# Exponentials of a decoder's attention as powers on GpSimd, and block limits in two-source steps on VectorE

## The chip, the cores and the metric
The kernel runs on one core of one Trainium2 chip. The metric is the device time of one execution in microseconds, the median of several runs. The engines of the core work from queues of their own and meet at semaphores: TensorE (PE in the profile), VectorE (DVE), ScalarE (ACT), GpSimd (POOL), and SyncE (SP), which issues the DMAs.

## The reference
A decoder of two layers works on `x`, 4 sequences of 512 rows with 512 features. Layer 0 is a state-space mixer, a cross attention over `ctx` and a feed-forward on selected rows. Layer 1 is what the change touches:

```python
# L1 attention: x is read as (seq=4, batch=512, hidden): 4 positions for each of 512 columns
scores = einsum('bhqd,bhkd->bhqk', q, k) / sqrt(32)      # 16 heads of 32, 4 key/value heads
scores = where(causal, scores, -inf)
attn   = einsum('bhqk,bhkd->bhqd', softmax(scores), v)
x = x + attn @ weight_proj.T
# L1 cross step: each block of 128 features of layernorm(x) is rounded to fp8 by its own limit
amax = max(abs(block)); safe = maximum(amax, 1e-4)
q    = (block * (448 / safe)).astype(float8_e4m3fn);   x = x + (q * safe / 448) @ quantised(ctx).T
# L1 feed-forward: rows rounded to int8, weights ternary
x = x + bitlinear(silu(bitlinear(n, w1)) * bitlinear(n, w3), w2)
```

Because the reference reads the first axis as time, attention has only four positions. A row of sequence s attends to s + 1 keys, and with 16 heads it has 16, 32, 48 or 64 scores.

## The kernel before, in words
`x` lies in SBUF as 16 tiles of 128 rows by 512 features. The last stages (from about 736 us to the end of the span) do the whole of layer 1 as one software pipeline. Tiles are taken in the order of `order`, so that tile n has position s = n % 4. Every engine runs one loop of NT + 15 = 31 turns (NT is 16), and in each turn it does a fixed list of steps on tiles of different age: in VectorE's loop `t2` is the tile two turns behind, `t3` the next older one, and so on. GpSimd's and ScalarE's loops count seven turns later, so their `t9` is the tile that VectorE calls `t2`. No planner orders this at run time. The list of steps in each loop is the order, and an instruction that waits holds everything behind it in its engine's queue.

The way of one tile: `turn_du` and `qkv_product` (PE), `keep_qkv` (ACT, L2185), the products of queries and keys on VectorE (`attend_scores`, L1576) for even positions and on GpSimd (`attend_odd`, L2681) for odd ones. Then `attend_softmax` on VectorE: a sum over 32 features (L1588), the largest score of each head (L1591), and the difference (L1594), which gives the third `at_step`. ScalarE's `exp_keys` (L2191) waits for that and writes the exponentials, which `at_exp` signals. `attend_weights` on VectorE waits for `at_exp`, sums them (L1602), inverts (L1605) and multiplies (L1607). In VectorE's list two steps stand between the difference and `attend_weights`: `add_down` (L1727) and `add_to_x(t3, "attended")` (L1632), the latter on the product of the attention that TensorE made for the tile before. Behind `attend_weights` stands `e_fp8` (L1280 to L1288), whose result ScalarE scales (`scale_eu`, L2256) and TensorE turns (`turn_eu`, L466). Then come the next turn's `f_scale`, `f_gate`, `attend_add`, `h_scale`, `e_scales`, `attend_scores` and so on.

GpSimd's list in one turn is: `minus_mean(t7, 0)`, `minus_mean(t12, 2)`, `minus_mean(t10, 1)` (all L2726), `deviation(t12, 2)` (L2734 and a power, L2737), `attend_part(t9, 1)` (L2702), `deviation(t7, 0)`, `attend_begin` (L2692), `attend_part(t9, 2)`, `deviation(t10, 1)`, `attend_part(t9, 3)`, `attend_last` (L2710), `f_gains` (L2747), `attend_odd`, `h_gain`, `e_back`. `minus_mean(t10, 1)` waits for `x_attended`, which is signalled by the `add_to_x(t3, "attended")` that stands in VectorE's list directly ahead of `attend_weights`. TensorE's list is `e_product`, `turn_o`, `f_down`, `attend_out`, `f_up`, half of `qkv_product`, `turn_eu`, the other half, `turn_du`.

The limits of the fp8 blocks are made in `e_scales` on VectorE: the largest magnitude of each of four blocks (L1643), times the row's scale and not under 1e-4 (L1647, a one-source step), a reciprocal (L1649), and times the scale and 448 (L1651, one-source). All four write 128x4 or less.

ScalarE works with tables of functions: where the next function is not in the loaded table, the program has an ACT_TABLE_LOAD. In the last stages the functions are Exp (L2191), Silu (L2210), Square, Identity and Copy.

Of the kernel before, what the change touches and what calls it, by code (L numbers as in the profile page):

```python
# [13 lines left out]
ALU = mybir.AluOpType  # L14
ACT = mybir.ActivationFunctionType
# [3 lines left out]
P = 128  # L19
BATCH, SEQ, D = 4, 512, 512  # L20
NT = BATCH * SEQ // P
TPB = SEQ // P
KD = D // P
# [12 lines left out]
AH, AKV, AHD = 16, 4, 32  # L36
# [4 lines left out]
ASCALE = float(AHD) ** -0.5  # L41
# [5 lines left out]
FP8_MAX = 448.0  # L47
# [15 lines left out]
def behind(n, lags):  # L63

    return [n - lag if 0 <= n - lag < NT else None for lag in range(lags)]
# [77 lines left out]
def decoder_kernel(nc, x_in, ctx_in, ctxT_in, mask_in, win_in, wout_in, d_in, dtb_in, alog_in, bw_in, cw_in,  # L143
                   lnw_in, lnb_in, wr_in, br_in, w1_in, b1_in, w2_in, b2_in, wqkv_in, wproj_in,
                   f1_in, f2_in, f3_in, out):
    with ExitStack() as top:
        signals = {}

        def sig(name):
            name = HANDED_ON.get(name, (name, 0))[0]  # L150
            if name not in signals:
                signals[name] = top.enter_context(nc.semaphore(name))
            return signals[name]
# [11 lines left out]
        fixed = Region(nc, -(-nc.sbuf_base // 32) * 32, top_end)  # L165
        x = fixed.ring("x", NT, [P, D])
        ident, ones = fixed.one("ident", [P, P]), fixed.one("ones", [P, 1])
        mhalf = fixed.one("mhalf", [P, 8])
        b_sum = fixed.one("b_sum", [P, NT])


# [202 lines left out]
        def spread(name, number, shape, dt=F32, parts=work):  # L374

            made = []
            for k in range(number):
                part = next(p for p in parts if p.end - p.at >= Region.room(p, shape, dt) or p is parts[-1])
                made.append(part.one(f"{name}_{k}", shape, dt))
            return made  # L380
# [9 lines left out]
        at = spread("at", 1, [P, 3, BATCH * AH])[0]  # L390
# [21 lines left out]
        def grouped(ap):  # L412
            return ap.rearrange("p (g r d) -> p g r d", g=AKV, r=R)
# [566 lines left out]
        def vector_program(e):  # L980
            w, own = Waits(e, sig), Steps()
# [216 lines left out]
            for i in range(1, NT + 2):  # L1198
                m, k = i - 1, i - 2
# [435 lines left out]
            def e_scales(n):  # L1635


                rstd = d_mv[1][n % 2][:, 3:4]
                lim, inv = (am[:, k, :] for k in range(2))
                w.wait_ge("e_centred", n + 1)  # L1640
                if n:
                    w.wait_ge("eu_ready", n)
                e.tensor_reduce(lim, eu[n % 2][:].rearrange("p (g n) -> p g n", n=P), AX.X, ALU.max,  # L1643
                                apply_absolute_value=True).then_inc(sig("vector_step"), 1)
                w.wait_ge("vector_step", own.next())
                w.wait_ge("e_rstd", 2 * n + 2)
                e.tensor_scalar(lim, lim, rstd, 1e-4, ALU.mult, ALU.max).then_inc(sig("vector_step"), 1)  # L1647
                w.wait_ge("vector_step", own.next())
                e.reciprocal(inv, lim).then_inc(sig("vector_step"), 1)  # L1649
                w.wait_ge("vector_step", own.next())  # L1650
                e.tensor_scalar(inv, inv, rstd, FP8_MAX, ALU.mult, ALU.mult).then_inc(sig("e_scales"), 1)  # L1651

            def e_fp8(n):
                w.wait_ge("eu_scaled", n + 1)
# [77 lines left out]
            for n in range(NT + 15):  # L1732
                t0, t1, t2, t3, t4, t5, t6, t7, t8, t9, t10, t11, t12, t13, t14, t15 = behind(n, 16)
# [59 lines left out]
        def scalar_program(e):  # L1793
            w = Waits(e, sig)
# [154 lines left out]
            for i in range(1, NT + 2):  # L1949
                m, k = i - 1, i - 2  # L1950
# [234 lines left out]
                e.activation(qkv[n % 6][:, h * QKV // 2:(h + 1) * QKV // 2],  # L2185
                             banks.of["qkv", n, h][:, 0:QKV // 2], ACT.Copy).then_inc(sig("qkv_ready"), 1)

            def exp_keys(n):
                low, expd = (at[:, k, 0:(n % BATCH + 1) * AH] for k in (1, 2))
                w.wait_ge("at_step", 6 * n + 3)  # L2190
                e.activation(expd, low, ACT.Exp, scale=ASCALE).then_inc(sig("at_exp"), 1)  # L2191

            def high_oT(n):
                w.wait_ge("o_turned", n + 1)
                w.wait_ge("attended", n)
                e.activation(oT_hi[:], banks.of["o", n][:], ACT.Copy).then_inc(sig("oT_ready"), 1)
# [62 lines left out]
            def f_round(n):  # L2259
                w.wait_ge("f_scale", n + 1)  # L2260
                e.activation(fu[:], fu[:], ACT.Copy, bias=MAGIC, scale=fm[n % 12][:, 3:4]).then_inc(
                    sig("f_rounded"), 1)

            def high_proj():
                w.wait_ge("w_loaded", 32)
                e.activation(wproj_hi[:], wproj[:], ACT.Copy).then_inc(sig("wproj_hi"), 1)
# [36 lines left out]
            for n in range(NT + 15):  # L2303
                t0, t1, t2, t3, t4, t5, t6, t7, t8, t9, t10, t11, t12, t13, t14, t15 = behind(n, 16)
                if t13 is not None:
                    f_round(t13)
                if t11 is not None:
                    e_centre(t11)
                if t13 is not None:
                    f_quantise(t13)  # L2310
                if t9 is not None:
                    keep_qkv(t9, 0)
                    keep_qkv(t9, 1)
                if n == 3:
                    high_proj()
                if t14 is not None:
                    h_round(t14)
                if t10 is not None:
                    high_oT(t10)
                if t8 is not None:  # L2320
                    high_du(t8)
                if t11 is not None:
                    scale_eu(t11, 1, "e_scales", "eu_scaled")
                if t12 is not None:
                    square(t12, 2)
                    f_centre(t12)
                if t9 is not None:
                    exp_keys(t9)
                if t14 is not None:
                    h_quantise(t14)  # L2330
                if t10 is not None:
                    square(t10, 1)
                if t7 is not None:
                    square(t7, 0)
                if t13 is not None:
                    silu(t13, 0)
                    silu(t13, 1)
                if t11 is not None:
                    scale_eu(t11, 2, "e_back", "eu_ready")
                if t13 is not None:  # L2340
                    silu(t13, 2)
                if t7 is not None:
                    d_normal(t7)
                if t11 is not None:
                    keep_eT(t11)


        def gpsimd_program(e):
            w = Waits(e, sig)
# [334 lines left out]
            def weights(n, t):  # L2684
                return at[:, 0, t * AH:(t + 1) * AH].rearrange("p (g r) -> p g r", g=AKV).unsqueeze(3) \
                    .broadcast_to([P, AKV, R, AHD])

            def attend_begin(n):
                w.wait_ge("at_step", 6 * n + 6)
                if n >= 2:  # L2690
                    w.wait_ge("o_turned", n - 1)
                e.tensor_tensor(grouped(o[n % 2][:]), shared(n - n % BATCH, (R + 1) * AHD), weights(n, 0),  # L2692
                                ALU.mult).then_inc(sig("o_begun"), 1)

            def attend_part(n, t):
                if t > n % BATCH:
                    return
                turn = PVS[n] + t - 1
                w.wait_ge("at_step", 6 * n + 6)
                if turn >= 2:  # L2700
                    w.wait_ge(*pv_added[turn - 2])
                e.tensor_tensor(grouped(pv[turn % 2][:]), shared(n - n % BATCH + t, (R + 1) * AHD), weights(n, t),  # L2702
                                ALU.mult).then_inc(sig("pv_ready"), 1)
# [51 lines left out]
            def h_gain(n):  # L2755
                m = fm[n % 12]
                w.wait_ge("h_scale", n + 1)
                if n >= 12:
                    w.wait_ge("x_done", n - 11)
                e.tensor_scalar(m[:, 10:11], m[:, 7:8], fs[:, 9:10], 1.0 / 127.0, ALU.mult, ALU.mult).then_inc(  # L2760
                    sig("h_gain"), 1)

            w.wait_ge("blk_ready", BATCH)
            w.wait_ge("ternary", 3 * QUARTERS)
            for n in range(NT + 15):
                t0, t1, t2, t3, t4, t5, t6, t7, t8, t9, t10, t11, t12, t13, t14, t15 = behind(n, 16)
                if t7 is not None:
                    minus_mean(t7, 0)
                if t12 is not None:
                    minus_mean(t12, 2)  # L2770
                if t10 is not None:
                    minus_mean(t10, 1)
                if t12 is not None:
                    deviation(t12, 2)
                if t9 is not None:
                    attend_part(t9, 1)
                if t7 is not None:
                    deviation(t7, 0)
                if t9 is not None:
                    attend_begin(t9)  # L2780
                    attend_part(t9, 2)
                if n == 8:
                    low_proj()
                if t10 is not None:
                    deviation(t10, 1)
                if t9 is not None:
                    attend_part(t9, 3)
                    attend_last(t9)
                if t12 is not None:
                    f_gains(t12)  # L2790
                if t8 is not None:
                    attend_odd(t8)
                if t15 is not None:
                    h_gain(t15)
                if t10 is not None:
                    e_back(t10)
# [182 lines left out]
```

## Time and profile before
| what | us |
|---|---|
| time, median of 3 runs | 1078.13 |
| lowest, highest | 1075.67, 1079.51 |
| span of the profiled execution, first to last instruction | 1077.4 |
| PE busy | 1038.9 (96%) |
| DVE busy | 842.1 (78%) |
| ACT busy | 637.9 (59%) |
| POOL busy | 474.5 (44%) |

The page gives no other time of the profiled execution than its span. The span is 0.7 us under the median of the timed runs and within their spread. The shares are means over stages with different limits, so the stage that the change touches has to be read by itself. In the rows, a number in brackets with an arrow is the time for which the engine sat idle before that instruction, and what ended it.

### The profile page before, as it was taken

What the parts mean: (1) busy time and instruction counts of PE and PEld (TensorE: products, weight loads), DVE (VectorE), ACT (ScalarE), POOL (GpSimd) and SP (SyncE); (2) the same over time, 40 slices, a digit from 0 to 9 for tenths busy, and PEclk for the clock granted to TensorE, in tenths of its full rate; (3) what the DMA queues carried; (4) which work ended last, traced back from release to release, by engine and by line L of the source; (5) the groups of instructions that cost most, each with busy time, mean ns of one, the idle gap of its engine ahead of it and who ended that gap; (6) DMA issues with size and microseconds to landing.
All of it is one profiled execution on the core that took longest, in us unless ns stands there. A gap on an engine that the chain in (4) does not pass through costs nothing.

```text
span 1077.4 us, 15310 instructions
## 1 busy us (share of the span) xinstructions
PE 1038.9 (96%) x5161; PEld 775.2 (72%) x5161; DVE 842.1 (78%) x1595; ACT 637.9 (59%) x1241; POOL 474.5 (44%) x720
## 2 busy tenths in 40 slices
PE   8999999999999999999999999999899999999998
PEld 7777788778878888676566787877676666666544
DVE  6787767777768667746988868786888989989975
ACT  5743444344443443336566557764568989989774
POOL 6444424432343323425888652005554554735411
PEclk9999999999999999999999999999999999999999
DMA  8300000000000000207110036410001121112122
GB/s 295 118 1 1 1 1 2 1 1 1 1 1 1 1 2 1 81 14 301 75 40 2 1 116 260 145 47 1 1 6 24 42 34 39 42 34 52 34 57 76
DMA packets 46446, 52.46 MB, mean 49 GB/s; under 512 B 32545, under 2 KB 33569, under 8 KB 44065
## 3 DMA queue, kind: packets, MB, share of 16 engines
q1 hardware_dynamic: 46368, 51.49, 14.9%
q8 instruction: 41, 0.67, 0.2%
q14 instruction: 37, 0.30, 0.1%
HBM read 39.92 MB, written 4.19 MB: 41 GB/s over the span
## 4 chain that ended last, share of the span: by engine, by line
PE 62%; DVE 21%; ACT 8%; issue 6%; POOL 3%; DVEq 0%; ACTq 0%; POOLq 0%
PE bank L458 45%; PE bank L466 4%; PE bank L554 4%; PE bank L947 3%; DVE cum_h L1073 2%; PE bank L545 1%; PE bank L472 1%; DVE y L1109 1%; PE bank L535 1%; DVE ctx_lo L1325 1%; DVE at L1588 1%; ACT squares L2230 1%; DVE prod L1576 1%; DVE state L1124 1%; DVE wgt L1081 1%
## 5 line engine op out<-in xcount | busy, mean ns | idle before, releaser
L458 PE MATMUL bank<-win_hi,a_uT_hi 128*128 128x512 f32 (+1 forms) x320 | 126.7, 396 | 3.9 <-DVE win_lo L1024 3.0
L458 PE MATMUL bank<-win_lo,a_uT_hi 128*128 128x512 f32 (+1 forms) x320 | 120.2, 376 | 0.0
L458 PE MATMUL bank<-win_hi,a_uT_lo 128*128 128x512 f32 (+1 forms) x320 | 119.7, 374 | 0.0
L1857 ACT ACTIVATE ex<-bank 128x16 f32<-128x16 f32 (+1 forms) x16 | 3.0, 189 | 140.0 <-PE bank L510 140.0
L2469 POOL TENSOR_TENSOR y<-y,off 128x512 f32<-128x512 f32 x24 | 38.0, 1585 | 105.5 <-DVE off L1094 105.5
L458 PEld LDWEIGHTS bank<-win_hi,a_uT_hi 128*128 128x128 f32 x320 | 60.6, 189 | 17.8 <-DVE win_lo L1024 4.8
L458 PEld LDWEIGHTS bank<-win_lo,a_uT_hi 128*128 128x128 f32 x320 | 60.7, 190 | 12.5 <-issue 2.4
L458 PEld LDWEIGHTS bank<-win_hi,a_uT_lo 128*128 128x128 f32 x320 | 60.5, 189 | 11.4
L554 PEld LDWEIGHTS bank<-xs,wgt 128*128 128x128 f32 x512 | 61.1, 192 | 6.8 <-issue 5.7
L458 PE MATMUL bank<-f,fqT_next 128*128 128x512 fp8e4 (+1 forms) x312 | 64.0, 362 | 0.0
L1081 DVE SCALAR_TENSOR_TENSOR wgt<-wgt,cb 128x512 f32<-128x512 f32 x64 | 54.0, 846 | 10.9 <-ACT wgt L1886 10.7
L458 PE MATMUL bank<-wq,eT 128*128 128x512 f32 x128 | 59.7, 611 | 2.3 <-ACT eT L2201 2.3
L554 PE MATMUL bank<-xs,wgt 128*128 128x64 f32 x512 | 60.9, 272 | 0.3 <-ACT wgt L1886 0.3
L458 PE MATMUL bank<-wq,b_uT 128*128 128x512 f32 x128 | 57.6, 593 | 0.0
L1073 DVE TENSOR_TENSOR cum_h<-cum,eye_h 64x512 fp32r<-64x512 f32 x64 | 55.7, 908 | 1.4 <-ACT cum L1876 0.9
L1848 ACT ACTIVATE zs<-bank 128x512 f32<-128x512 f32 x32 | 18.8, 587 | 61.3 <-PE bank L458 61.3
L458 PEld LDWEIGHTS bank<-f,fqT_next 128*128 128x128 bf16 x312 | 29.7, 98 | 33.1 <-issue 2.8
L2394 POOL TENSOR_SCALAR sq<-sq 128x2 f32<-128x2 f32 x16 | 3.2, 199 | 112.6 <-ACT cs L1822 112.5
L458 PE MATMUL bank<-wout_hi,yT_hi 128*128 128x512 f32 x128 | 51.9, 405 | 0.7 <-DVE yT_lo L1146 0.7
L458 PE MATMUL bank<-wout_lo,yT_hi 128*128 128x512 f32 x128 | 50.5, 395 | 0.0
L458 PE MATMUL bank<-wout_hi,yT_lo 128*128 128x512 f32 x128 | 50.5, 394 | 0.0
L458 PE MATMUL bank<-wqkv_hi,d_uT_hi 128*128 128x384 f32 x128 | 45.7, 357 | 0.3 <-DVE d_uT_lo L1569 0.3
(360 smaller groups left out, 3172.8 us busy)
## 6 DMA issues: line engine op xcount, KB each, us to landing
wchunk<-w_in SPq DMA_DIRECT2D x32, 256.0 KB, 6.4
stage<-f_in SPq DMA_DIRECT2D x3, 1408.0 KB, 7.3
x<-x_in SPq DMA_DIRECT2D x16, 256.0 KB, 6.2
land<-win_in SPq DMA_DIRECT2D x4, 1024.0 KB, 7.2
wq<-ctxT_in SPq DMA_DIRECT2D x4, 1024.0 KB, 6.5
out<-x SPq DMA_DIRECT2D x16, 256.0 KB, 2.0
ctx<-ctx_in SPq DMA_DIRECT2D x3, 1024.0 KB, 4.7
first_stage<-f_in SPq DMA_DIRECT2D x2, 1408.0 KB, 13.0
```

What stands on the lines that cost most here:

```text
L458: made = e.matmul(bank, a, b, start=start and n == 0, stop=stop and n == len(pairs) - 1)
L466: made = e.transpose(bank[:, k * P:(k + 1) * P], src[:, k * P:(k + 1) * P], idn[:])
L472: e.matmul(bank[:, 0:P], ident[:], ident[:], start=True, stop=True)
L535: e.matmul(bank[:], cum_s[q // 2][rows, :], cum_h[q][rows].rearrange("p a b -> p (a b)"), start=True, stop=True).then_inc(sig("decay_summe ...
L545: e.matmul(bank[:], cT[:], state[:, n * 512:(n + 1) * 512], start=True, stop=True).then_inc(sig("off_done"), 1)
L554: made = e.matmul(bank[:, j * HD:(j + 1) * HD], wgt[h // HG][:, h % HG, :], xs[m % 2][:, h * HD:(h + 1) * HD], start=True, stop=True)
L947: made = e.matmul(bank[:], hqT[n % 2][:, k * P:(k + 1) * P], f2[:, k, :], start=k == 0, stop=k == KH - 1)
L1073: e.tensor_tensor(cum_h[q][rows], cum[rows, :].bitcast(F32).unsqueeze(1).broadcast_to([P // 2, HG, P]), eye_h[rows, first:first + HG].unsq ...
L1081: e.scalar_tensor_tensor(out=wgt[q][:], in0=wgt[q][:], scalar=1.0, in1=cb[:].unsqueeze(1).broadcast_to([P, HG, P]), op0=ALU.min, op1=ALU.m ...
L1109: e.tensor_tensor(part, part, zs[m % 2][:, cols], ALU.mult).then_inc(sig("y_gated"), 1)
L1848: e.activation(zs[i % 2][:, n * 512:(n + 1) * 512], banks.of["proj_z", i, 3 + n][:], ACT.Tanh, scale=0.5).then_inc(sig("z_tanh"), 1)
L2469: e.tensor_tensor(y[m % 2][:, cols], y[m % 2][:, cols], off[:], ALU.add).then_inc(sig("y_off"), 1)
```

## The change
Four things change in the last stages. `exp_keys` leaves ScalarE and becomes a GpSimd step: a constant, exp of 1/sqrt(32), is raised to the power of the difference. It stands behind `minus_mean` and `deviation(t12, 2)` and ahead of `attend_part(t9, 1)`. The two one-source steps of `e_scales` become scalar_tensor_tensor, whose second tensor is one column of a constant spread over four. The three constants are written once by GpSimd. `mhalf` shrinks from 8 columns to 4 and `rows` takes a place of the same size.

```diff
-        mhalf = fixed.one("mhalf", [P, 8])
+        mhalf, rows = fixed.one("mhalf", [P, 4]), fixed.one("rows", [P, 4])
+        key_base, least, largest = (rows[:, k:k + 1] for k in range(3))
...
-                e.tensor_scalar(lim, lim, rstd, 1e-4, ALU.mult, ALU.max).then_inc(sig("vector_step"), 1)
+                w.wait_ge("rows_set", 1)
+                e.scalar_tensor_tensor(out=lim, in0=lim, scalar=rstd, in1=least.broadcast_to([P, KD]), op0=ALU.mult,
+                                       op1=ALU.max).then_inc(sig("vector_step"), 1)
...
-                e.tensor_scalar(inv, inv, rstd, FP8_MAX, ALU.mult, ALU.mult).then_inc(sig("e_scales"), 1)
+                e.scalar_tensor_tensor(out=inv, in0=inv, scalar=rstd, in1=largest.broadcast_to([P, KD]), op0=ALU.mult,
+                                       op1=ALU.mult).then_inc(sig("e_scales"), 1)
...
-            def exp_keys(n):
-                low, expd = (at[:, k, 0:(n % BATCH + 1) * AH] for k in (1, 2))
-                w.wait_ge("at_step", 6 * n + 3)
-                e.activation(expd, low, ACT.Exp, scale=ASCALE).then_inc(sig("at_exp"), 1)
...
-                if t9 is not None:
-                    exp_keys(t9)
...
+            def exp_keys(n):
+
+                size = (n % BATCH + 1) * AH
+                w.wait_ge("at_step", 6 * n + 3)
+                e.tensor_tensor(at[:, 2, 0:size], key_base.broadcast_to([P, size]), at[:, 1, 0:size], ALU.pow).then_inc(
+                    sig("at_exp"), 1)
...
+            for part, value in ((key_base, np.exp(ASCALE)), (least, 1e-4), (largest, FP8_MAX)):
+                made = e.memset(part, float(value))
+            made.then_inc(sig("rows_set"), 1)
+            w.wait_ge("rows_set", 1)
...
                 if t9 is not None:
+                    exp_keys(t9)
                     attend_part(t9, 1)
```

## Rows read from the trace of the kernel before
**Rows 1.** Windows per tile: stretch, length, busy PE, PEld, DVE, ACT, POOL (instructions), clock, DMA, GB/s
```profile
876.10:895.00 18.90, 18.90 (x92) 12.49 (x91) 15.36 (x36) 17.05 (x33) 7.51 (x16) 1.00 0.27 42
...
913.90:933.60 19.70, 19.70 (x97) 12.72 (x95) 19.15 (x39) 17.49 (x33) 12.13 (x19) 1.00 0.16 36
```
**Rows 2.** Timeline of VectorE: start, length, line, tiles; first and last L1602, one tile's
```profile
741.15 0.17 DVE L1602 TENSOR_REDUCE ax<-at 128x16 f32<-128x16 f32 x1 [0.28 <-ACT at L2191]
...
913.93 0.20 DVE L1602 TENSOR_REDUCE ax<-at 128x16 f32<-128x48 f32 x1
...
917.00 0.69 DVE L1288 TENSOR_TENSOR eu<-eu,et 128x512 f32<-128x512 f32 x1
...
1009.52 0.26 DVE L1602 TENSOR_REDUCE ax<-at 128x16 f32<-128x64 f32 x1
```
**Rows 3.** Waits from 760 us to the end: who for whom, total us, times, longest
```profile
DVE x L1632 <- PE bank L458: 17.1, 18, 2.0
...
DVE f_h L1686 <- ACT f_h L2210: 5.0, 5, 2.0
...
PE bank L466 <- ACT eu L2256: 3.6, 7, 0.9
...
PE bank L458 <- ACT eT L2201: 2.3, 3, 0.8
```
**Rows 4.** Timeline of TensorE: `f_up`, a wait, and one product at two levels of the clock
```profile
761.02 0.47 PE L458 MATMUL bank<-wproj_hi,oT_hi 128*128 128x512 f32 x1 [1.93 <-DVE oT_lo L1623]
...
913.12 4.93 PE L458 MATMUL bank<-f,fqT 128*128 128x512 fp8e4 x24
...
1017.22 5.37 PE L458 MATMUL bank<-wq,eT 128*128 128x512 f32 x8 [0.78 <-ACT eT L2201]
...
1034.24 3.67 PE L458 MATMUL bank<-wq,eT 128*128 128x512 f32 x8 [0.78 <-ACT eT L2201]
```
**Rows 5.** Lines view by shape, ScalarE: loads and exponentials (busy, mean ns)
```profile
L2191 ACT ACT_TABLE_LOAD x12 | 15.4, 1283 | 0.2
L2210 ACT ACT_TABLE_LOAD x12 | 15.4, 1283 | 0.2
...
L2191 ACT ACTIVATE at<-at 128x64 f32<-128x64 f32 x4 | 1.0, 256 | 3.5 <-DVE at L1594 3.5
```
**Rows 6.** Powers and a product on GpSimd, by line: ns least/median/most
```profile
L2737 POOL TENSOR_TENSOR e_mv<-e_mv,mhalf x16: 548/549/1005, 756.8 to 1031.3; 128x1 f32<-128x1 f32 x16
...
L2396 POOL TENSOR_TENSOR sq<-sq,mhalf x16: 706/725/784, 24.0 to 427.2; 128x2 f32<-128x2 f32 x16
...
L2384 POOL TENSOR_TENSOR a_rs<-a_rs,mhalf x5: 576/1006/1540, 28.7 to 294.9; 128x4 f32<-128x4 f32 x3, 128x1 f32<-128x1 f32 x1, 128x3 f32<-128x3 f32 x1
...
L2412 POOL TENSOR_TENSOR dt<-dt,nega x16: 217/620/2162, 27.2 to 430.9; 128x16 f32<-128x16 f32 x16
```
**Rows 7.** Timeline of GpSimd around the same L1602
```profile
914.09 0.19 POOL L2726 TENSOR_SCALAR e_mv<-e_mv 128x1 f32<-128x1 f32 x1 [5.07 <-DVE e_mv L1632]
...
914.63 0.86 POOL L2737 TENSOR_TENSOR f_mv<-f_mv,mhalf 128x1 f32<-128x1 f32 x1
```
**Rows 8.** Timeline of ScalarE: the scaling ahead of the turn that TensorE waits for
```profile
918.61 1.27 ACT L2256 ACTIVATE eu<-eu,am 128x128 f32<-128x128 f32 x4
```
**Rows 9.** VectorE's small and two-source steps, by line: ns least/median/most
```profile
L1647 DVE TENSOR_SCALAR am<-am,e_mv x16: 229/348/1234, 757.4 to 1037.1; 128x4 f32<-128x4 f32 x16
...
L1651 DVE TENSOR_SCALAR am<-am,e_mv x16: 229/603/1090, 758.8 to 1037.6; 128x4 f32<-128x4 f32 x16
...
L1286 DVE TENSOR_TENSOR eu<-eu,et x16: 692/1470/1476, 768.5 to 1042.0; 128x512 f32<-128x512 f32 x16
...
L1081 DVE SCALAR_TENSOR_TENSOR wgt<-wgt,cb x64: 669/686/1787, 37.3 to 461.2; 128x512 f32<-128x512 f32 x64
```
**Rows 10.** A step of L1647 beside the GpSimd instruction of that moment
```profile
905.24 1.23 DVE L1647 TENSOR_SCALAR am<-am,e_mv 128x4 f32<-128x4 f32 x1
...
905.16 1.28 POOL L2681 TENSOR_TENSOR prod<-qkv,qkv 128x512 f32<-128x512 f32 x1 [3.00 <-ACT qkv L2185]
```

## The prediction
> **What bounds the kernel now.** I read the page's busy shares first: TensorE is busy 96% of the span, so a gain elsewhere is worth nothing unless TensorE waits for it. The change lives in the last stages, so I cut these into windows, one for each tile of attention, from one L1602 (the first step of `attend_weights`) to the next. Sixteen of them run from 741.15 to 1009.52 us [rows 2]. In the window between a tile of one key and a tile of two TensorE is busy 18.90 of 18.90 us and VectorE 15.36. In a window that ends with a tile of four keys it is 19.70 of 19.70, and VectorE 19.15 [rows 1]. So TensorE sets a period of 18.9 us, and VectorE stands 0.5 to 3.5 us behind it. Third, the waits from 760 us on: VectorE waits 18 times for a product that L1632 adds, 17.1 us in all, and 5.0 us for ScalarE's Silu. That is the room there is on VectorE: some 0.95 us a wait. ScalarE is busy 17 of 18.9 us [rows 1], and TensorE waits for it 3.6 us at L466 and 2.3 at L458 [rows 3].
>
> **Exponentials leave ScalarE.** In these stages 12 loads of the Exp table and 12 of the Silu table take 15.4 us each [rows 5]. With no Exp between the Silus one load is left, so 23 x 1.283 = 29.5 us go, and 16 exponentials of about 0.24 us (0.256 at 64 columns [rows 5]) with them: 33 us of ScalarE's time, 2.6 us of each full period. Since TensorE has little idle time, what this can give back is its waits for ScalarE, 3.6 + 2.3 = 5.9 us [rows 3]. I put nothing in the sum for it, and keep a gain of 6 us as the bound.
>
> **The power on GpSimd.** The trace has no power wider than 4 columns, so I take the undisturbed durations: 548 ns for one column, 706 for two, 1006 for four (the median of L2384, three of whose five have four columns) [rows 6]. That is (1006 - 548) / 3 = 153 ns for each column and 395 ns fixed. I take it as a line. 16 columns are then 2.84 us, 32 are 5.29, 48 are 7.74 and 64 are 10.19, together 26.06 us for four tiles and 104.2 us for sixteen. The other end is the product on GpSimd, 217 ns for 16 columns [rows 6]: if the columns of a power beyond the first few cost as little, each power takes some 0.7 us. I choose the line because the step from column to column is the same from 1 to 2 (158) and on to 4 (150), with no sign of flattening.
>
> The Trainium skill, "GPSIMD Engine Reference", section 3.1, counts about 2.6 cycles an element for a two-input step on GpSimd, which it measured on an add. No row here shows a power at that rate. By that rule the powers would cost almost what one column costs, and the result is the first rival below.
>
> **What is late, and who waits.** Before, the exponential ran beside `add_down` and `add_to_x`, which stand in VectorE's list between the difference and L1602 (913.93) [rows 2]. After, it can't start there. It stands on GpSimd behind `minus_mean(t10, 1)`, which waits for the very `add_to_x` that ends as L1602 could start: at 914.09, after 5.07 us of idle. Behind that come L2734 and a power of one column (914.63; 0.55 undisturbed, 0.86 here) [rows 7]. So it starts at 914.63 + 0.55 + 0.08 = 915.26, 1.33 us behind L1602's old start, and with 0.1 us to hand over, VectorE stands still for 1.43 us + the power in every turn. Behind it in VectorE's queue are `e_fp8`, which gives TensorE its next `turn_eu`, and all steps of the next turn. None of that is hidden.
> Tiles 3 to 15: 13 x 1.43 = 18.6, and powers of 104.2 - (2.84 + 5.29 + 7.74) = 88.3: 106.9 us. Tiles 1 and 2 have no L2734 in front: 2 x 0.5 + 5.29 + 7.74 = 14.0. Tile 0 has a free GpSimd but sets off the chain of its `o` later; I take 2 of its 2.84 us. Sum 123 us.
>
> **Does another engine take some of it back?** During the stall TensorE has only `f_up` (from 913.12, 4.93 us [rows 4]) and half of the projection, about 7 us. It ends near L1602 + 6.1, as before, and then waits for `turn_eu`, which needs `e_fp8`. Counted from the end of the stall, `turn_eu` can start at + 5.25: `e_fp8` ends 3.76 us behind L1602 (917.69 [rows 2]), ScalarE takes 1.27 [rows 8], and I add 0.2 for the hand-overs. The rest of TensorE's list is 18.9 - 4.93 - 2.1 = 11.9 us, the add 0.7: 17.9 us. VectorE's own list takes 15.4 to 19.2 us [rows 1], and part of the 15.4 has to wait for TensorE. So what follows the stall takes 18 to 19 us, within 1 us of the old period. So VectorE's stall adds to the period in full: the sum takes no credit. An estimate of the two small corrections, ScalarE's waits gone (-5) and TensorE's clock (below, + 5 to + 25), is kept for the range.
> GpSimd's later steps are due the same time after the stall as before, and it is busy 7.5 to 12.1 us of a period [rows 1], so it doesn't become the bound by its sum of work. It does so by its place in the chain.
>
> **The limits' steps.** L1647 and L1651 take 229 ns undisturbed and 1234 and 1090 at most [rows 9]. The step of 1.23 us at 905.24 ends at 906.47, and the GpSimd product of 905.16 ends at 906.44 [rows 10], so it waited for GpSimd to finish. Does the two-source form avoid this? Two-source steps of VectorE from SBUF stretch as well: L1286 from 692 to 1476, and the scalar_tensor_tensor of L1081 from 669 to 1787 [rows 9]. I take 0: the wait stays. The ends are a gain of the whole stretch, (0.649 + 0.566 - 0.46) x 16 = 12 us by the means of the same two lines, and a loss of 3 us if the new form takes 0.1 us more each. The Trainium skill, "SBUF — State Buffer", section "Who interferes with whom", says that a VectorE instruction with two SBUF inputs contends with a GpSimd instruction that reads SBUF. By that rule the new form would wait as the old one did, beside every product of GpSimd.
> The three memsets run before GpSimd's wait for `blk_ready` and the new waits on `rows_set` are met long before: 0, and if that cover were gone, under 1 us once. The smaller `mhalf` costs nothing.
>
> **The sum.** 1077.4 + 123 = 1200.4 us of span. The span is 0.7 us under the median of the timed runs. I say 1200 us.
>
> **Rivals.**
> 1. *A power costs little per column* (0.7 us at any width). For it: products do so on GpSimd [rows 6]. Against it: the line from 1 to 4 columns. Then each turn still stalls 1.43 + 0.7 = 2.1 us, 31 us in all, from which go up to 17.1 us in which VectorE waited for TensorE anyway and 5.0 for ScalarE [rows 3]: + 9 to + 20, so 1093 us.
> 2. *The clock.* TensorE would be idle for the stall less about 0.9 us in each turn, 3 to 11 us. It fell back to the 1.2 GHz level for part of the work behind its longer waits: the eight matmuls of `e_product` took 5.37 us at 1017.22, where it had little to do before, against 3.67 at 1034.24, both with 0.78 us of idle directly ahead [rows 4], 1.7 us lost. If each of 15 turns loses that and it all lands in the chain, + 25: 1225 us. If the low level lasts through more of the 12 us behind `turn_eu`, + 3 us or more a turn: up to 1250. For it: the waits are longer than the 1.93 us of 761.02, which is the longest of these stages. Against it: ahead of a tile of four keys VectorE's list is longer than TensorE's and hides 1 us or more.
> 3. *Faster.* The place is L1602: if the stall is no longer than what VectorE waits for TensorE at L1632, about 0.95 us, it costs nothing, and the 33 us freed on ScalarE remove TensorE's short waits for it, 5.9 us in all: 1072 us [rows 3]. This decides only if the exponential is there within 0.95 us of L1602's old start. Its start alone is 1.33 us behind, so this would need GpSimd's steps ahead of it to be faster than in [rows 7] too.
> 4. *The power flattens in part*, say 100 ns a column beyond four: 70% of the powers' 104 us: 1165 us.
>
> **How the numbers follow.** Line as read, small corrections: 0.68, 1190 to 1215. Rival 2: 0.12. Rival 4: 0.07. Rival 1: 0.08. Rival 3: 0.03, and 0.02 for no change. For 8 in 10 the range takes the forecast's case and half each of rivals 2 and 4, and their neighbourhood: 1140 to 1235 us. A measurement of this kernel tells 0.3%, 3 us, from no change. Faster 0.03, same 0.02, slower 0.95.
>
> **What will show it.** Right: in the profile after, the power's row reads about 2.8, 5.3, 7.7 and 10.2 us for 16, 32, 48 and 64 columns; the wait of L1602 for it heads VectorE's waits with about 120 us over 16 times; windows from L1602 to L1602 have lengths that follow the keys, about 23, 26, 28 and 31 us where they begin with 1, 2, 3 and 4 keys; one table load is left behind 736 us; the chain of waits has the power's line with about 9% of the span. L1647 and L1651 still have rows over 1 us. TensorE is idle ahead of `turn_eu`. Wrong: the power under 2 us at 64 columns, or windows that don't depend on the number of keys, or a wait of L1602 well below the power's duration, which would mean that GpSimd started it earlier than I say.

## The result, and the profile after
The changed kernel takes 1212.8 us (median of 4 runs, 1211.4 to 1215.7) against 1078.8 us of the kernel before on the same chip: a ratio of 1.125, 95% interval 1.123 to 1.127. The forecast was 1200 us, the range 1140 to 1235. The profiled execution has a span of 1213.6 us, 136.2 more than before. Line numbers moved by one to a few lines: L1603 is what L1602 was (first step of `attend_weights`), L1633 is L1632, L467 is L466, and the power is L2689.

The page's first parts of the kernel after: busy time and share of each engine, then TensorE's busy tenths and clock in 40 slices, then the shares of the chain that ended last, by engine and by line.
```profile
span 1213.6 us, 15291 instructions
...
PE 1065.0 (88%) x5161; PEld 798.3 (66%) x5161; DVE 847.0 (70%) x1595; ACT 607.6 (50%) x1202; POOL 584.4 (48%) x739
...
PE   8999999999999999999999998568776867786598
...
PEclk9999999999999999999999999778887988888899
...
PE 57%; DVE 19%; POOL 12%; ACT 7%; issue 5%; ACTq 0%; POOLq 0%; DVEq 0%
PE bank L459 41%; POOL at L2689 9%; PE bank L467 5%; PE bank L555 3%; PE bank L948 3%; DVE cum_h L1074 2%; PE bank L473 1%; ACT eu L2255 1%; DVE et L1284 1%; PE bank L546 1%; DVE eu L1289 1%; DVE y L1110 1%; DVE eu L1287 1%; PE bank L536 1%; DVE x L1633 1%
```
The loss is all in the last 40% of the slices: TensorE falls from 9 to 5 to 8 tenths there, and its clock with it. Its whole busy time rose by only 26 us. The new name in the chain is the power, with 9% of the span.

The power's rows by shape (busy us, mean ns of one), then who waited for whom from 760 us on (total us, times, longest), then ScalarE's table loads of the last stages.
```profile
L2689 POOL TENSOR_TENSOR at<-rows,at 128x64 f32<-128x64 f32 x4 | 42.1, 10534 | 0.0
L2689 POOL TENSOR_TENSOR at<-rows,at 128x48 f32<-128x48 f32 x4 | 32.1, 8015 | 0.0
...
L2689 POOL TENSOR_TENSOR at<-rows,at 128x32 f32<-128x32 f32 x4 | 21.7, 5432 | 0.0
...
L2689 POOL TENSOR_TENSOR at<-rows,at 128x16 f32<-128x16 f32 x4 | 11.6, 2910 | 1.6 <-DVE at L1595 1.6
```
```profile
ACT eu L2255 <- DVE eu L1289: 128.5, 14, 14.4
DVE ax L1603 <- POOL at L2689: 120.5, 15, 11.7
PE bank L467 <- ACT eu L2255: 108.3, 14, 13.0
```
```profile
L2209 ACT ACT_TABLE_LOAD x1 | 1.3, 1283 | 0.0
```
These rows answer to [rows 3, 5 and 6]. From 16 to 64 columns a power grows from 2.91 to 10.53 us, 159 ns a column. The waits are one wait seen three times down the chain: VectorE for the power, ScalarE for VectorE's `e_fp8` behind it, TensorE for ScalarE's scaled tile. 23 of 24 table loads are gone, and little had waited for ScalarE: VectorE 5.0 us for the Silu, TensorE 5.9 us in all [rows 3].

One stall, on GpSimd and on VectorE at a tile of four keys, as [rows 2 and 7] showed the place before. L1595 is the difference.
```profile
1020.36 0.19 POOL L2730 TENSOR_SCALAR e_mv<-e_mv 128x1 f32<-128x1 f32 x1 [5.48 <-DVE e_mv L1633]
1020.63 0.19 POOL L2738 TENSOR_SCALAR f_mv<-f_mv 128x1 f32<-128x1 f32 x1
1020.90 0.55 POOL L2741 TENSOR_TENSOR f_mv<-f_mv,mhalf 128x1 f32<-128x1 f32 x1
1021.42 10.54 POOL L2689 TENSOR_TENSOR at<-rows,at 128x64 f32<-128x64 f32 x1
```
```profile
1018.78 0.22 DVE L1595 TENSOR_TENSOR at<-at,ax 128x64 f32<-128x64 f32 x1
...
1020.19 0.08 DVE L1633 DVE_READ_ACCUMULATOR2_ANT e_mv<- 128x1 f32 x1
1031.99 0.26 DVE L1603 TENSOR_REDUCE ax<-at 128x16 f32<-128x64 f32 x1 [11.71 <-POOL at L2689]
```
The differences had been there since 1019.0. GpSimd starts on them at 1021.42, and VectorE stands still for 11.71 us, which is the power and 1.2 us of queue.

### The profile page after: what moved, and what is told of

Read it like the earlier page. It is cut to its first block, busy times and chain, and to the rows that moved or that the text cites. A ratio compares the mean times of both kernels' runs of the same rounds, so it can differ in the third digit from the quotient of the medians.

```text
span 1213.6 us, 15291 instructions
## 1 busy us (share of the span) xinstructions
PE 1065.0 (88%) x5161; PEld 798.3 (66%) x5161; DVE 847.0 (70%) x1595; ACT 607.6 (50%) x1202; POOL 584.4 (48%) x739
## 4 chain that ended last, share of the span: by engine, by line
PE 57%; DVE 19%; POOL 12%; ACT 7%; issue 5%; ACTq 0%; POOLq 0%; DVEq 0%
PE bank L459 41%; POOL at L2689 9%; PE bank L467 5%; PE bank L555 3%; PE bank L948 3%; DVE cum_h L1074 2%; PE bank L473 1%; ACT eu L2255 1%; DVE et L1284 1%; PE bank L546 1%; DVE eu L1289 1%; DVE y L1110 1%; DVE eu L1287 1%; PE bank L536 1%; DVE x L1633 1%
## 5 line engine op out<-in xcount | busy, mean ns | idle before, releaser
L459 PE MATMUL bank<-win_hi,a_uT_hi 128*128 128x512 f32 (+1 forms) x320 | 126.7, 396 | 3.9 <-DVE win_lo L1025 3.0
L459 PE MATMUL bank<-win_lo,a_uT_hi 128*128 128x512 f32 (+1 forms) x320 | 120.0, 375 | 0.0
L459 PE MATMUL bank<-win_hi,a_uT_lo 128*128 128x512 f32 (+1 forms) x320 | 119.7, 374 | 0.0
L467 PE MATMUL bank<-ident,eu 128*128 128x128 f32 x64 | 15.6, 392 | 108.3 <-ACT eu L2255 108.3
L2689 POOL TENSOR_TENSOR at<-rows,at 128x16 f32<-128x16 f32 (+3 forms) x16 | 107.6, 6723 | 1.6 <-DVE at L1595 1.6
L2255 ACT ACTIVATE eu<-eu,am 128x128 f32<-128x128 f32 x128 | 40.7, 393 | 128.6 <-DVE eu L1289 128.5
L1603 DVE TENSOR_REDUCE ax<-at 128x16 f32<-128x16 f32 (+3 forms) x16 | 3.3, 205 | 123.6 <-POOL at L2689 123.6
L467 PEld LDWEIGHTS bank<-ident,eu 128*128 128x128 f32 x64 | 10.1, 195 | 112.5 <-issue 78.2
L459 PEld LDWEIGHTS bank<-win_hi,a_uT_hi 128*128 128x128 f32 x320 | 60.6, 189 | 17.8 <-DVE win_lo L1025 4.8
L459 PEld LDWEIGHTS bank<-win_lo,a_uT_hi 128*128 128x128 f32 x320 | 60.6, 189 | 12.5 <-issue 2.4
L459 PEld LDWEIGHTS bank<-win_hi,a_uT_lo 128*128 128x128 f32 x320 | 60.4, 189 | 11.5
L459 PE MATMUL bank<-wq,eT 128*128 128x512 f32 x128 | 63.6, 643 | 2.3 <-ACT eT L2200 2.3
L459 PE MATMUL bank<-f,fqT_next 128*128 128x512 fp8e4 (+1 forms) x312 | 64.0, 362 | 0.0
L459 PE MATMUL bank<-wq,b_uT 128*128 128x512 f32 x128 | 57.6, 592 | 0.0
L459 PE MATMUL bank<-wqkv_hi,d_uT_hi 128*128 128x384 f32 x128 | 53.2, 416 | 0.3 <-DVE d_uT_lo L1570 0.3
```

What stands on the lines that cost most here:

```text
L459: made = e.matmul(bank, a, b, start=start and n == 0, stop=stop and n == len(pairs) - 1)
L467: made = e.transpose(bank[:, k * P:(k + 1) * P], src[:, k * P:(k + 1) * P], idn[:])
L2255: made = e.activation(block, block, ACT.Copy, scale=am[:, row, k:k + 1])
L2689: e.tensor_tensor(at[:, 2, 0:size], key_base.broadcast_to([P, size]), at[:, 1, 0:size], ALU.pow).then_inc(sig("at_exp"), 1)
```

## The experiments
Each was timed beside the kernel before on one chip, and its ratio is to that kernel.

**The limits' steps alone.** The changed kernel with `exp_keys` back where it was on ScalarE.
```diff
             def exp_keys(n):
...
-                e.tensor_tensor(at[:, 2, 0:size], key_base.broadcast_to([P, size]), at[:, 1, 0:size], ALU.pow).then_inc(
-                    sig("at_exp"), 1)
+                e.activation(expd, low, ACT.Exp, scale=ASCALE).then_inc(sig("at_exp"), 1)
```


> The changed kernel with the exponentials back on ScalarE, so only the two-source limit steps differ from the kernel before. My account (the two-source form waits for GpSimd just as the one-source form did, and its steps cost 221 instead of 229 ns undisturbed): 1078 us, within 3, and rows of both steps over 1 us. Rival (the new form is free of GpSimd): both lines fall to 0.22 us in every row, 12 us less VectorE time, and up to 6 us off the whole, 1072 us.


Measured: 1076.1 us, ratio 1.000 (0.9985 to 1.0014). Its rows of the two steps (ns least/median/most):
```profile
L1649 DVE SCALAR_TENSOR_TENSOR am<-am,e_mv,rows x16: 223/352/1239, 755.4 to 1033.5; 128x4 f32<-128x4 f32 x16
...
L1654 DVE SCALAR_TENSOR_TENSOR am<-am,e_mv,rows x16: 222/598/1093, 756.8 to 1034.0; 128x4 f32<-128x4 f32 x16
```
They are the rows of before almost number for number (348 and 603 in the middle, 1234 and 1090 at most, [rows 9]). A long one stood beside a product of GpSimd, and the two ended together:
```profile
979.20 1.28 POOL L2685 TENSOR_TENSOR prod<-qkv,qkv 128x512 f32<-128x512 f32 x1 [3.02 <-ACT qkv L2189]
...
979.25 1.24 DVE L1649 SCALAR_TENSOR_TENSOR am<-am,e_mv,rows 128x4 f32<-128x4 f32 x1
```
The two-source form buys nothing, and costs nothing, within 0.15%.

**The powers alone.** The changed kernel with both `tensor_scalar` steps of before.


> The changed kernel with the one-source limit steps of the kernel before, so only the powers on GpSimd differ. My account (all of the change is the power): 1213 us, within 3. Rival (the two-source steps add to VectorE's list, which now paces the stages, through waits for a busier GpSimd): 1205 us or less.


Measured: 1211.3 us, ratio 1.125 (1.123 to 1.127), the changed kernel's own ratio. So the whole change of time is the power's, within the 0.2% that the interval leaves.

**A subtraction in the power's place.** Same queue, same operands, same wait.
```diff
-                e.tensor_tensor(at[:, 2, 0:size], key_base.broadcast_to([P, size]), at[:, 1, 0:size], ALU.pow).then_inc(
+                e.tensor_tensor(at[:, 2, 0:size], key_base.broadcast_to([P, size]), at[:, 1, 0:size], ALU.subtract).then_inc(
```


> The changed kernel with a subtraction in place of the power, in the same place and with the same operands (the attention's weights are then other numbers). My account: 0.2 to 0.3 us at any width, a stall of some 1.7 us a turn, of which VectorE's old waits for TensorE take 1 us or more: 1080 to 1092 us. Rival (the place in the queue and the freed ScalarE matter more than the power's length): 1120 us or more, or under 1075 if the freed ScalarE gives back what TensorE waited.


Measured: 1088.8 us, ratio 1.011 (1.008 to 1.014). Its row of L2689 and VectorE's wait for it:
```profile
L2689 POOL TENSOR_TENSOR at<-rows,at x16: 213/254/294, 737.7 to 1016.2; 128x16 f32<-128x16 f32 x4, 128x32 f32<-128x32 f32 x4, 128x48 f32<-128x48 f32 x4, 128x64 f32<-128x64 f32 x4
```
```profile
DVE ax L1603 <- POOL at L2689: 20.1, 16, 1.5
```
GpSimd takes 0.21 to 0.29 us for what the power takes 2.9 to 10.5. The 20.1 us of waits that are left are the queue (1.2 us a turn) and the subtraction itself, and 12 us reach the end (1.1% of 1077). So of the 134 us, some 122 come with the power's duration, what a long stall does to TensorE's clock among them, and 12 with its place. VectorE's waits for TensorE at L1633, which this expectation had counted on, took almost none of the stall: from the first L1603 to the end they are 17.8 us, and 19.2 in the kernel before. What shrank is VectorE's wait for the Silu (2.0 against 5.0 us) and its own busy time (278.9 against 282.0).

**The power first in GpSimd's turn.**
```diff
+                if t9 is not None:
+                    exp_keys(t9)
                 if t10 is not None:
                     minus_mean(t10, 1)
...
                 if t9 is not None:
-                    exp_keys(t9)
                     attend_part(t9, 1)
```


> The changed kernel with the power ahead of the mean that waits for the attention product, so GpSimd starts it as soon as the differences are there. My account (VectorE stands still from the product's add to the power's end): the 1.4 us of queueing go and 1.3 to 2 us of the power run beside the two adds, 2.8 to 3.4 us a turn over 14 turns: 1168 to 1175 us, and the wait of L1603 falls from 120 to about 80 us. Rival (GpSimd's queue does not matter, the power's length alone does, or what is now behind the power is late in its turn): 1205 us or more.


Measured: 1167.1 us, ratio 1.084 (1.082 to 1.087), 1 us under the foot of what was expected. The wait of L1603 is 80.2 us in 14 waits, against 123.6 in 16 in the changed kernel, first tile included: 43 us less wait, 45.7 us less time. What stands ahead of a long instruction in a queue costs its own length and the cover that it forgoes.

**The weights behind `e_fp8`,** on top of that.
```diff
-                if t2 is not None:
-                    attend_weights(t2)
                 if t4 is not None:
                     e_fp8(t4)
+                if t2 is not None:
+                    attend_weights(t2)
```


> The kernel with the power first in GpSimd's turn, and VectorE's `attend_weights` behind `e_fp8` instead of ahead of it. If the loss is only that VectorE's queue stands still behind the wait: 3 us of `e_fp8` now cover each power and TensorE gets its turn of `eu` before the stall: 40 to 45 us less than 1167, so 1122 to 1130 us, and the wait of L1603 falls from about 80 to 35 to 45 us. Rival (the later weights delay GpSimd's values and the next turn's adds by as much): 1150 us or more.


Measured: 1143.2 us, ratio 1.062 (1.060 to 1.064). 24 us gained, not 40, and L1603 still waits 54.6 us where 35 to 45 were expected, so this expectation missed. The rows of L1603 and of L1619 (the adds of the next turn), first of the kernel with the power first, then of this one (busy, mean ns, idle before and releaser):
```profile
L1603 DVE TENSOR_REDUCE ax<-at 128x16 f32<-128x64 f32 x4 | 1.0, 258 | 37.0 <-POOL at L2689 37.0
...
L1603 DVE TENSOR_REDUCE ax<-at 128x16 f32<-128x16 f32 x4 | 0.7, 170 | 4.1 <-POOL at L2689 3.8
...
L1619 DVE TENSOR_TENSOR o<-o,pv 128x512 f32<-128x512 f32 x20 | 15.0, 751 | 2.2 <-POOL o L2696 2.2
```
```profile
L1603 DVE TENSOR_REDUCE ax<-at 128x16 f32<-128x64 f32 x4 | 1.0, 258 | 28.0 <-POOL at L2689 28.0
...
L1603 DVE TENSOR_REDUCE ax<-at 128x16 f32<-128x16 f32 x4 | 0.7, 163 | 3.0 <-POOL at L2689 3.0
...
L1619 DVE TENSOR_TENSOR o<-o,pv 128x512 f32<-128x512 f32 x20 | 19.9, 993 | 9.3 <-POOL o L2696 9.3
```
The cover was (37.0 - 28.0) / 4 = 2.25 us a turn, not 3: with GpSimd inside the power, `e_fp8` itself runs 0.7 us shorter (its four lines, 35.8 us for 16 tiles against 47.0). For tiles of one key next to nothing was left to cover. And 7 us came back as a wait of the next turn's adds for GpSimd's values, with 5 us more in the adds and 4 us more in VectorE's waits for the Silu (6.8 against 2.8). The rival named this mechanism; it was a part of the miss, not the whole.

**Filler matmuls ahead of `turn_eu`,** in the changed kernel, to hold TensorE's clock through the stall.
```diff
-                if n in (0, 1, NT - 3):
-                    keep_busy(bank, 6)
+                if n < NT - 2:
+                    keep_busy(bank, (26, 50, 74, 98)[(n + 2) % BATCH])
```


> The changed kernel with filler matmuls of 128 columns on TensorE ahead of each turn of `eu`: 26, 50, 74 or 98 of them by the number of keys, which fill about 2.7, 5.2, 7.7 and 10.2 us of the idle time there. If the 12.6 us that the changed kernel took beyond its stalls are the clock's (granted clock 0.78 to 0.93 of full in the windows): the clock reads 0.95 to 1.0 and the time falls to 1200 to 1206 us. Rival (they are VectorE's own list and its waits for a busier GpSimd): the clock rises, the time stays at 1210 us or more.


Measured: 1274.9 us, ratio 1.183 (1.181 to 1.185). It told nothing on the clock: one call is two instructions of 0.115 us for fp32, so 50 fillers took 11.3 us where 5.7 were idle, and TensorE itself was late. I took the fillers first for ones in the neighbouring tile's stall, and moved them:


> As the first filler kernel, whose counts belonged to the neighbouring tile, now 24, 46, 70 or 92 filler matmuls by the stall that they stand in (0.115 us each as measured: 2.8, 5.3, 8.0, 10.6 us, against idle times of 3.1, 5.7, 8.3 and 11 to 12 us). If the 12 us beyond the stalls are the clock's: granted clock 0.98 or more, 1200 to 1206 us. Rival (VectorE's own list): the clock rises as well, the time stays at 1209 us or more.


Measured: 1273.8 us, ratio 1.183 (1.181 to 1.186), no better, since length and place were now both wrong. The third try has the first one's places and half its counts, 12, 23, 34 and 45:


> As the two filler kernels before, whose fillers were twice as long as counted (one matmul of 128 fp32 columns is two instructions): now 12, 23, 34 or 45 filler matmuls, 24 to 90 instructions of 0.115 us, 2.8, 5.3, 7.8 and 10.4 us by the stall that they stand in, against idle times of 3.1, 5.7, 8.3 and 11 to 12 us. If the 12 us beyond the stalls are the clock's: granted clock 0.98 or more, 1200 to 1206 us. Rival (VectorE's own list): the clock rises as well, the time stays at 1209 us or more.


Measured: 1194.2 us, ratio 1.109 (1.107 to 1.112), 6 us under the foot of the range expected, because that took the 12 us beyond the stalls for the whole of the clock's share. It is 18.6 us under the changed kernel by the medians, 17 by the ratios of each to the kernel before on its own chip, at equal stalls: L1603 waits 123.5 us in the one and 123.6 in the other. The turn of `eu` behind a stall of a three-key tile, in the changed kernel and with the last 49 of its 68 filler instructions (start, length):
```profile
1004.67 1.09 PE L467 MATMUL bank<-ident,eu 128*128 128x128 f32 x4 [8.29 <-ACT eu L2255]
```
```profile
983.77 5.63 PE L473 MATMUL bank<-ident 128*128 128x128 f32 x49
990.01 0.66 PE L467 MATMUL bank<-ident,eu 128*128 128x128 f32 x4 [0.61 <-ACT eu L2255]
```
Windows between two stalls, the same tiles in the changed kernel, and 80 us with the fillers (stretch, length, busy PE, PEld, DVE, ACT, POOL, clock, DMA, GB/s):
```profile
970.20:999.40 29.20, 20.95 (x91) 14.40 (x91) 17.83 (x35) 14.62 (x29) 17.05 (x19) 0.88 0.12 27
999.40:1032.00 32.60, 21.64 (x91) 15.04 (x91) 19.84 (x37) 14.62 (x29) 22.75 (x21) 0.82 0.11 24
```
```profile
940.00:1020.00 80.00, 78.34 (x466) 58.66 (x465) 48.99 (x98) 40.45 (x81) 50.85 (x52) 1.00 0.13 29
```
The granted clock right behind that stall, in the changed kernel and with the fillers (same columns):
```profile
1004.67:1005.80 1.13, 1.13 (x5) 1.13 (x6) 1.13 (x3) 1.03 (x3) 0.96 (x3) 0.50 0.00 0
1005.80:1008.00 2.20, 2.20 (x8) 2.20 (x8) 2.20 (x4) 2.20 (x4) 1.88 (x3) 0.50 0.00 0
```
```profile
990.01:990.70 0.69, 0.69 (x6) 0.69 (x7) 0.69 (x2) 0.69 (x2) 0.69 (x1) 1.00 0.00 0
```
Behind a stall the four turns take 1.09 us instead of 0.66, at half the full clock, which is the 1.2 GHz level. The mean clock of these two windows is 0.82 and 0.88; over all windows from 744.7 us on it lies between 0.76 and 1.00, 0.87 in the mean, and 0.97 with the fillers, a little under the 0.98 expected. The time from the first L1603 to the end shrinks from 468.9 to 450.8 us, 18.1. Only the fillers differ, so TensorE's clock is worth 17 to 19 us of the loss: shown. In VectorE's trace the 18 us lie in its waits for products at L1633 (28.1 us against 18.7), in those at L1624 (4.8 against 3.1), and in its own busy time, 287.3 against 281.0: with TensorE late, more of VectorE's steps run longer (L1577, L1654).

**Is there anything to win by freeing ScalarE?** The kernel with the power first, and the subtraction in its place:


> The kernel with the power first in GpSimd's turn, and a subtraction in place of the power (the attention's weights are then other numbers): what a power that costs almost nothing would give. If freeing ScalarE gives back what TensorE waited for it: 1068 to 1073 us. Rival (TensorE's own list sets the pace, and ScalarE had been out of the way): 1075 to 1080 us.


Measured: 1073.3 us, ratio 0.9965 (0.995 to 0.998). This is what a free exponential would give: 3.8 us, 0.35%, at the upper edge of what was expected. TensorE's waits for ScalarE, from 760 us on, answer to the 3.6 and 2.3 us of [rows 3]:
```profile
PE bank L459 <- ACT eT L2200: 2.3, 3, 0.8
PE bank L467 <- ACT eu L2255: 1.0, 2, 0.7
```
The one went down by 2.6 us, the other did not move, with 31 us less of ScalarE's time. The kernel computes other weights, so it is a bound and no version.

**An exponential from Silu's table.** In the kernel before, ScalarE makes tanh(x / 2) and 1 - t, VectorE the rest:
```diff
-                e.activation(expd, low, ACT.Exp, scale=ASCALE).then_inc(sig("at_exp"), 1)
+                e.activation(expd, low, ACT.Tanh, scale=ASCALE / 2).then_inc(sig("at_tanh"), 1)
+                w.wait_ge("at_tanh", n + 1)
+                e.activation(expd, expd, ACT.Copy, scale=-1.0, bias=1.0).then_inc(sig("at_exp"), 1)
...
                 w.wait_ge("at_exp", n + 1)
+                e.reciprocal(expd, expd).then_inc(sig("vector_step"), 1)
+                w.wait_ge("vector_step", own.next())
+                e.tensor_scalar(expd, expd, 2.0, -1.0, ALU.mult, ALU.add).then_inc(sig("vector_step"), 1)
```


> The kernel before with the exponential made of a hyperbolic tangent on ScalarE, exp(x) = 2 / (1 - tanh(x / 2)) - 1, in the table that Silu uses: one table load is left of 24, for one more small step on ScalarE (0.2 us) and two on VectorE (0.5 us) a turn. My account (TensorE sets the pace, its waits for ScalarE were 5.9 us in all, VectorE is near the bound before a tile of four keys): 1071 to 1077 us, 0.1 to 0.5% under the kernel before. Rival (VectorE's two steps cost in the chain what the loads gave): 1077 to 1082 us.


Measured: 1082.2 us, ratio 1.005 (1.003 to 1.006): slower by 4 us, and my account missed; the rival's upper edge is what came. From 736 to 1000 us, this kernel and then the one before (columns as above):
```profile
736.00:1000.00 264.00, 253.36 (x1239) 175.55 (x1238) 232.80 (x499) 188.84 (x403) 138.59 (x233) 1.00 0.13 28
```
```profile
736.00:1000.00 264.00, 255.23 (x1236) 175.93 (x1235) 228.92 (x465) 212.03 (x411) 137.19 (x233) 0.99 0.13 28
```
ScalarE is 23 us freer, VectorE 4 us busier, and TensorE did less in the same time. From 760 us on TensorE waits longer for the scaled tile than the 3.6 us before [rows 3], and the two steps, which stand ahead of `e_fp8`, are the likely cause:
```profile
PE bank L467 <- ACT eu L2263: 6.6, 6, 2.1
```
With VectorE's two steps moved between the two adds:


> The kernel with the exponential made of a hyperbolic tangent, its two steps on VectorE now between the two adds, where VectorE waits up to 2 us for TensorE. If the 4 us of the first form were these steps behind the wait: 1075 to 1079 us. Rival (they delay the add of the attention product instead): 1081 us or more.


Measured: 1079.2 us, ratio 1.002 (1.001 to 1.003), at the upper edge of what was expected; that wait of TensorE is 5.0 us here. The place of the two steps was worth 0.3%, and half a microsecond a turn on VectorE outweighs 2.3 on ScalarE. No version tried that computes the right weights beats the kernel before.

## Why the prediction was right, by its steps
- *The power's line.* From 1, 2 and 4 columns it gave 2.84, 5.29, 7.74 and 10.19 us; measured are 2.91, 5.43, 8.02 and 10.53. It was 3% short at 64 columns. The line rested on the shortest of three powers of four columns in the kernel before (rows below), and there is luck in that: from 1.53 us the slope would have been 327 ns a column and the powers twice as long. What spoke for the short one was the step from one column to two, 158 ns. All 16 take 107.6 us, where it had 104.2. Rivals 1 and 4 fell with that row. The Trainium skill, "GPSIMD Engine Reference", section 3.1, gives about 2.6 cycles an element for two inputs. The subtraction is of that small order (81 ns for 48 more columns), the power is not, at 159 ns a column.
```profile
77.02 1.01 POOL L2384 TENSOR_TENSOR a_rs<-a_rs,mhalf 128x4 f32<-128x4 f32 x1
183.38 1.53 POOL L2384 TENSOR_TENSOR a_rs<-a_rs,mhalf 128x4 f32<-128x4 f32 x1
294.90 1.54 POOL L2384 TENSOR_TENSOR a_rs<-a_rs,mhalf 128x4 f32<-128x4 f32 x1
```
- *What is late, and who waits.* The order behind `add_to_x`, and the stall of 1.43 us + the power, are in the trace: stalls of 4.09, 6.61, 9.19 and 11.71 us, the power and 1.2 each. The sum of stalls is 123.6 us against my 123, closer than its terms: the powers are 3.4 us longer, the queue 0.25 us shorter in each of 13 turns, and the first tile stalls 3.0 us where I took 2. The kernel with the power first moved as this account says, and the one with the subtraction lost 12 us where rival 1 had 15. One sign was named wrongly: I gave 23, 26, 28 and 31 us to the windows that begin with 1, 2, 3 and 4 keys, but the stall stands at a window's end. Between the tiles of four keys at 920.49 and 1031.99 the windows that end with 1, 2, 3 and 4 keys take 25.1, 24.7, 29.2 and 32.6 us; the one that begins with 4 keys is not the longest, it is the 25.1.
- *Does another engine take some of it back?* I put 0. Two terms that I left to the range are both real. From the first L1603 to the end, the changed kernel takes 468.9 us and the kernel before 336.2 [rows 2], 132.7 more, of which 120.5 are stalls. With the clock held by fillers it is 1191.5 - 740.7 = 450.8, 114.6 more, that is 5.9 less than the stalls. So the loss is the stalls, less 5.9, plus 18.1 for the clock. That the 5.9 equal my bound for TensorE's waits on ScalarE (5.9) is chance: 2.3 us of those waits, at L459 in the new numbering, are still there. VectorE's rows, from the first L1602 or L1603 to the end, in the kernel before and in the one with the fillers, show where most of it lies: its waits for the Silu fall from 5.0 to 2.0 us, its busy time by 1.0, its waits at L1576 and L1618 by 0.9 and 0.8, and those for TensorE at L1632 only from 19.2 to 18.7. The table loads are the likely cause of the first; no run here separates it.
- *Rival 2, the clock,* was priced 25 us with a chance of 0.12, as if it stood against the forecast. It came in with 17 to 19 us beside it: the two were not rivals but terms of one sum. That is the step that was mis-sized: clock 0 where 18.1 was measured in the spans, other waits 0 where -5.9 was. Their sum is 12.2 of the 12.8 us by which 1200 fell short of 1212.8; that it is no more is luck, since two terms that I had both put at nothing offset each other in part. The change of time was forecast as 122 us and is 134.
- *The limits' steps* at 0 were right, within 0.15%. The Trainium skill, "SBUF — State Buffer", section "Who interferes with whom", has two SBUF inputs on VectorE contend with a GpSimd instruction that reads SBUF, and the step of 1.24 us beside the GpSimd product of 979.20 agrees. In the changed kernel both lines have such rows too, up to 1211 and 1328 ns.
- *Rival 3, faster,* asked that the exponential be there within 0.95 us. The subtraction placed first in GpSimd's turn met that, and gave 0.35%. The direction was right, the size 3.8 us where I had 6: of the 5.9 us that TensorE waited for ScalarE only 2.6 went.

## What to carry to other kernels
Price an operation by its width on the engine it moves to: a power of one column on GpSimd looks like any small step, and 64 columns cost 10.5 us. Then ask what is queued behind the one who waits, and price TensorE's clock behind each stall as a term of the sum, not as another outcome. An engine that is busy 90% is not thereby worth relieving: here 31 us less on ScalarE were worth 4.

## What the runs showed of the hardware that was not expected
- The power on GpSimd costs 159 ns a column of 128 rows, linear from 16 to 64 (2.91, 5.43, 8.02, 10.53 us), against 1.7 ns a column for a subtraction of the same operands.
- After eleven idle stretches of 5.7 to 13.0 us in the changed kernel TensorE's first work ran at the 1.2 GHz level (four turns in 1.08 to 1.12 us against 0.66, granted clock 0.50 behind that of 1004.67). After the three of 3.1 us it varied: 0.91, 0.63 and 0.80 us, with a granted clock of 1.00 behind the second. Fillers in all 14 gave back 17 to 19 us, about 1.3 us each.
- Tanh needs no table load beside Silu, Exp does (24 loads before [rows 5]): one load was left in the last stages of that kernel.
```profile
L2217 ACT ACT_TABLE_LOAD x1 | 1.3, 1283 | 0.0
```
